# Edge stage of a graph network layer: all sixteen feature products of a step behind block 0 of the next step

## The reference, cut to what matters

```
def head(w1, bb1, w2, bb2, a1, aab1, a2, aab2):
    feats = jnp.maximum(x @ w1 + bb1, 0.0) @ w2 + bb2           # 256 -> 256 -> 64
    x_cat = jnp.concatenate([feats[row], feats[col], elem[:, None]], axis=1)
    hid = jnp.maximum(x_cat @ a1 + aab1, 0.0)                    # 129 -> 129
    e1 = (hid @ a2 + aab2)[:, 0]
    ...                                                          # softmax over the edges of a row
x = _layernorm(x + _L0_gnn_ref(...))
x = _layernorm(x + _L1_gnn_ref(...))
```

## Time and profile before

| what | us |
|---|---|
| median of 3 runs | 3850.22 |
| lowest and highest of them | 3822.89, 3856.89 |
| span of the profiled execution | 3543.6 |
| TensorE matmuls busy in it | 3149.9 (89%) |
| VectorE busy | 2727.7 (77%) |
| ScalarE busy | 1885.7 (53%) |
| GpSimd busy | 1802.6 (51%) |

### The profile page before, as it was taken

How to read it: one execution, slowest core, us unless ns; L and a number is a source line. 1 busy time by engine, 2 the same in 40 slices (tenths; PEclk the granted TensorE clock), 3 DMA queues, 4 the chain that set the end, 5 groups by cost and what they waited for, 6 DMA issues and landing times. The chain is left out here.

```text
span 3543.6 us, 66445 instructions
## 1 busy us (share of the span) xinstructions
PE 3149.9 (89%) x15901; PEld 2168.2 (61%) x15901; DVE 2727.7 (77%) x9307; ACT 1885.7 (53%) x4499; POOL 1802.6 (51%) x1827
## 2 busy tenths in 40 slices
PE   4987879885999997699999999999999999995775
PEld 2455546553555554477777777777777777773333
DVE  4988879774554544588888888888888888887997
ACT  2455557663665655344444444444444444443886
POOL 0046656665777774544444444444444444421777
PEclk9999999998999998799999999999999999997998
DMA  5889996444666665333333333333333333322885
GB/s 156 291 309 307 312 327 192 156 157 144 221 210 211 207 208 204 124 116 118 118 116 114 113 115 116 118 118 118 118 116 114 118 118 118 115 69 87 271 270 195
DMA packets 288948, 596.16 MB, mean 168 GB/s; under 512 B 41262, under 2 KB 198746, under 8 KB 288886
## 3 DMA queue, kind: packets, MB, share of 16 engines
q1 hardware_dynamic: 212774, 362.51, 30.6%
q0 software_dynamic: 75744, 232.45, 20.2%
q10 hardware_dynamic: 368, 0.52, 0.0%
HBM read 287.39 MB, written 322.05 MB: 172 GB/s over the span
## 5 line engine op out<-in xcount | busy, mean ns | idle before, releaser
L1029 PE MATMUL bank<-w_node,xT 128*128 128x384 f32 x1564 | 597.2, 506 | 80.2 <-ACT bank L617 79.6
L1218 POOL TENSOR_TENSOR u_hc<-u_hc 128x1536 f32<-128x1536 f32 x98 | 270.3, 2758 | 756.7 <-DVE u_h L1328 732.5
L1440 PE MATMUL bank<-xh,w1h 128*128 128x512 f32 x1568 | 537.7, 424 | 18.8 <-DVE xl L1357 14.9
L1270 ACT ACTIVATE hidT<-bank,b1c 128x512 f32<-128x512 f32 x392 | 268.7, 685 | 530.4 <-PE bank L1440 530.4
L1440 PE MATMUL bank<-xh,w1l 128*128 128x512 f32 x1568 | 494.1, 396 | 0.0
L1440 PE MATMUL bank<-xl,w1h 128*128 128x512 f32 x1568 | 493.0, 396 | 0.0
L1351 DVE TENSOR_SCALAR hidT<-bank,b1c 128x512 f32<-128x512 f32 x392 | 293.6, 749 | 199.7 <-PE bank L1440 196.7
L1029 PEld LDWEIGHTS bank<-w_node,xT 128*128 128x128 f32 x1564 | 286.5, 196 | 247.3 <-ACT bank L617 98.6
L1454 PE MATMUL bank<-hidT,w2f 128*64 128x256 f32 x3136 | 381.7, 385 | 0.9 <-issue 0.9
L617 ACT ACTIVATE bank<-bias_all 128x512 f32<-128x512 f32 x391 | 235.2, 602 | 250.8 <-DVE H L727 244.5
L1366 DVE STREAM_TRANSPOSE feat<-catT 32x256 f32<-32x256 f32 x784 | 342.7, 437 | 17.1 <-ACT catT L1279 3.0
(11 more groups left out here) (273 smaller groups left out, 6525.3 us busy)
## 6 DMA issues: line engine op xcount, KB each, us to landing
hc_tab<-H SPq DMA_DIRECT2D x78, 960.0 KB
hc_tab<-zero_row SPq DMA_DIRECT2D x15, 4992.0 KB
er<-edge_tab SPq DMA_DIRECT2D x98, 512.0 KB, 4.1
X<-in_x SPq DMA_DIRECT2D x78, 640.0 KB
out_x<-O SPq DMA_DIRECT2D x78, 640.0 KB
edge_tab<-u_x SPq DMA_DIRECT2D x98, 256.0 KB, 2.2
edge_tab<-feat SPq DMA_DIRECT2D x98, 256.0 KB, 2.2
u_hc<-hc_tab,u_idx POOLq DMA_INDIRECT x392, 4.4
```

Source lines behind the costliest of these rows:

```text
L1029: ins = t_.matmul(p[:, 0:384], xT[i % XR][:, c * P:(c + 1) * P], w_node[:, c, :], start=False, stop=c == 1, skip_group_check=True)
L1218: g.tensor_tensor(c, c, u_hc[s][:, :, MULT:MULT + 3].unsqueeze(3).to_broadcast([P, 4, 3, P]), ALU.mult).then_inc(u_scaled, 1)
L1270: a.activation(hidT[m][:, :], bank[2 + m % 2][:, :], ACT.Relu, bias=b1c[:, m:m + 1])\
L1440: ins = t_.matmul(bank[2 + m % 2][:, :], w[:, c, m * P:(m + 1) * P], xx[s][:, c, :], start=n == 0, stop=n == 5)
```

## The change

TensorE's list has one piece, features_0_1, with lag 2 behind hidden_0; it does both halves of step u-1, and the piece features_0 between blocks 6 and 7 is gone. The waits for all relus of the step and for the banks stand once, ahead of the first half. The relu of block 0 on ScalarE overwrites hidT 0, which the first half of the step before now reads later; so this relu waits for w2_ready of that step's second half. On ScalarE the piece features_0 moves from the end of the list to the place ahead of features_1, with lag 3. VectorE, GpSimd and SyncE are as they were.

```diff
                 def relu(u, m):
                     act.wait_ge(w1_ready, u * 8 + (m + 1))
+                    if m == 0 and after(u, 1):
+                        act.wait_ge(w2_ready, u * 2)
                     a.activation(hidT[m][:, :], bank[2 + m % 2][:, :], ACT.Relu, bias=b1c[:, m:m + 1])\
                         .then_inc(act_hid, 1)
...
-                skewed(act, US, 2, [(relu_0, 2), (features_1, 3), (seed_0, 3), (root, 0), (relu_2, 2), (norm, 0),
-                                    (relu_4, 2), (seed_1, 3), (high, 1), (relu_6, 2), (features_0, 2)])
+                skewed(act, US, 2, [(relu_0, 2), (features_0, 3), (features_1, 3), (seed_0, 3), (root, 0), (relu_2, 2),
+                                    (norm, 0), (relu_4, 2), (seed_1, 3), (high, 1), (relu_6, 2)])
...
                 def features(u, k):
-                    pe.wait_ge(act_hid, u * 4 + 2 * k + 2)
-                    pe.wait_ge(dve_hid, u * 4 + 2 * k + 2)
-                    if after(u, 1):
-                        pe.wait_ge(cat_ready, u * 4 + 2 * k - 2)
+                    if k == 0:
+                        pe.wait_ge(act_hid, u * 4 + 4)
+                        pe.wait_ge(dve_hid, u * 4 + 4)
+                        if after(u, 1):
+                            pe.wait_ge(cat_ready, u * 4)
...
-                def features_1(u, s):
+                def features_0_1(u, s):
+                    features(u, 0)
                     features(u, 1)
...
-                skewed(pe, US, 2, [(hidden_0, 1), (features_1, 2), (hidden_1, 1), (hidden_2, 1), (scores_0, 2),
+                skewed(pe, US, 2, [(hidden_0, 1), (features_0_1, 2), (hidden_1, 1), (hidden_2, 1), (scores_0, 2),
                                    (hidden_3_4, 1), (turn, 0), (hidden_5, 1), (scores_1, 2), (hidden_6, 1),
-                                   (features_0, 1), (hidden_7, 1)])
+                                   (hidden_7, 1)])
```

More of the change, by code:

```diff
@@ L1494, in hidden_6 @@
                     hidden(u, s, 6)
-                def features_0(u, s):
-                    features(u, 0)
                 def hidden_7(u, s):
```

## The result

The changed kernel takes 3966.68 us (median of 4 runs, 3957.06 to 3995.11), the kernel before 3844.37. The ratio is 1.0336 with a 95% interval of 1.0292 to 1.038: 3.4% slower, about 129 us (the two medians alone differ by 122). The forecast was 4028, with a range from 3990; the direction and the mechanism were right, the size was too large by 61 us in time and by 49 in the difference (178 against 129).

A forecast was written before the change was run, and what follows sets the result against it. TensorE, busy without a pause in the edge stage, was taken as the bound: 17.98 - 0.20 + 1.76 + 0.29 = 19.83 us a step, in total +178 us on the median 3850.22, giving 4028 us, range 3990 to 4065.

The forecast's parts named there:

- Term 1: TensorE's merged product group: eight products (1.87 us) move, one change-over in and out goes away, gaining 0.20 us a step.
- the loop: Group's start to end of block 5 on TensorE, 12.60 us, then VectorE's stretch with signal, 6.93: 19.53 against 17.98.
- Term 3: ScalarE's queue behind the new wait: relu of block 0 starts later, seed_0 and scores_0 are late, 0.29 us a step.
- Sum: Edge stage: 1.84 us a step, x 96 = 177, with the ends 178, added to the median 3850.22: 4028 us.
- Term 2: TensorE ahead of the merged group: waits 1.76 us a step for VectorE's relu of block 7.
- What was moved past: Other work on VectorE, GpSimd and SyncE (feat_0, gate and u_var, norm, high, stores): costs nothing at 19.8 us a step.
- B: Rival: TensorE's pauses in the edge stage cost clock as well; over 1% slower, chance 0.05.

The follow-up runs named there:

- the version with both repairs: Changed kernel, each half of the products waiting for its own relus, ScalarE's relu of block 0 for the first half only: ratio 0.992, in another sitting 0.9893.
- The two edits of ScalarE's part: Changed kernel with ScalarE's seed_0 ahead of the relu of block 0: ratio 1.0365; or with that relu waiting for the first half only: 1.0276.

## Why the prediction was right or wrong

What bounds each step was forecast rightly, and the sum built on it came out too large. The steps that failed are three sizes: the group of Term 1 and of the loop, taken at 3.75 us where it measured 3.60; the late scores of Term 3, taken at 0.29 where they measured about 0.14; and the carry-over in Sum, which left the edge stage out of the 307 us between span and median.

**Term 2 was right.** The wait of 1.76 us for the relu of block 7 came out as 1.66 to 1.68 of idle time, plus the 0.10 of changing over, VectorE's stretch at 6.93, and the loop closes over it. Splitting the wait, shortening the stretch and lengthening it (0.89 for 0.89) all moved the time as this says.

**What was moved past** cost nothing that shows: 12.58 from the group's start to the end of block 5 and VectorE's 6.93 add up to the whole period of 19.51.

**B, the loss of clock**, didn't happen behind any pause of 1.66 to 1.68 us. In the four traces of the changed kernel it did happen behind four longer ones: one of 1.94 us in the middle of the stage, one of 2.38 in its first steps, one of 2.00 and one of 2.01 in its last. The last section has the numbers.

**The group was sized wrong (Term 1 and the 12.60 of the loop).** I took 1.87 us for eight products and doubled it. But 1.88 contains the way out of the group once: thirty-two records take 3.60 us (2201.26 to 2204.86), not 3.75, and 3.67 in the version with both repairs. So a change-over costs 0.10 + 0.10 and another 0.08 to 0.15 hidden in the group's length, 0.28 to 0.35 rather than 0.20. The repaired version shows it without any wait: 17.98 - 17.70 = 0.28. Why the group behind a pause is the shorter one wasn't examined. Worth 0.15 x 96 = 14 us.

**The late scores were sized wrong (Term 3).** 0.29 a step was forecast. ScalarE's relu starts 0.11 after the group's end where I had taken the 0.25 of the earlier trace rows, so seed_0 is that much earlier, and the late scores cost only about 0.14 on average of both forms of the step (12.58 from group to end of block 5, against 12.60 - 0.15 without them). The two edits of ScalarE's part gave 0.12 to 0.13 back. Worth 14 us.

**The carry-over to the median failed (Sum).** I saw 307 us between the span and the median and wrote that the edge stage has no part in them. It has some 16, by the one trace of the kernel before from where runs take 3844: it already loses them there through its thin spare time, the changed kernel hardly does, and that much of the new loss was there before. The sum corrected: 178 - 14 - 14 - 16 = 134, measured 132 between the two spans and 129 by the ratio. All three went the same way, and the lower end of the range, 38 us below the forecast, has room for each alone but not for 44. The rest of the 61 us isn't the change's: with its fourth run the kernel before has a median of 3844.37 and not 3850.22, and the ratio says 129 where the two medians say 122. That the range missed by 23 us is in part the luck of these draws.

## What to carry to other kernels

Before a piece of work is moved on the engine that bounds, look at which wait it stands ahead of: a product that needs nothing new is the cover of the wait behind it, and merging two groups should not merge their waits. Measure the spare time of every wait that ends just in time (here 0.32 us of 17.98), since it says what a change may cost and where the small delays of another sitting will show. And when the profiled span is far from the median, as the 3543.6 here from 3850.22, the profile may be of other conditions, and even a stage that looks insensitive to them may change, as this one did by some 16 us.

## What the runs showed of the hardware that was not expected

TensorE's granted clock fell at the end of some short pauses, or right behind them, and not at others of the same length. In the changed kernel with two more transposes the second group follows a pause of 3.19 us and took 6.46 us in place of 3.67; the granted clock over 1740 to 1747 was 0.58. It was 1.00 until 1739, then 0.50 until 1745, 0.59 over the next us and 1.00 over the one after. The groups behind it follow pauses of 2.56 to 2.58 us, nearly all alike. Most of them kept the full clock, but the one right behind took 5.10, and five more, spread over the stage from 2091 to 3504 us, took 5.02 to 5.06, at a granted clock of 0.74 to 0.77 over 6 us each:

```profile
1740.16 6.46 PE L1465 MATMUL bank<-hidT,w2f 128*64 128x256 f32 x32 [3.19 <-issue]
1763.38 5.10 PE L1465 MATMUL bank<-hidT,w2f 128*64 128x256 f32 x32 [2.58 <-issue]
1785.17 3.67 PE L1465 MATMUL bank<-hidT,w2f 128*64 128x256 f32 x32 [2.56 <-issue]
...
2091.22 5.02 PE L1465 MATMUL bank<-hidT,w2f 128*64 128x256 f32 x32 [2.57 <-issue]
...
2439.37 5.02 PE L1465 MATMUL bank<-hidT,w2f 128*64 128x256 f32 x32 [2.56 <-issue]
```

The changed kernel itself shows the same at still shorter pauses. In one trace a group behind 1.94 us took 5.36, with a granted clock of 0.72 over 2180 to 2186; in another a group behind 1.96 us took 3.67, at 1.00:

```profile
2180.07 5.36 PE L1457 MATMUL bank<-hidT,w2f 128*64 128x256 f32 x32 [1.94 <-issue]
```

```profile
2689.18 3.67 PE L1457 MATMUL bank<-hidT,w2f 128*64 128x256 f32 x32 [1.96 <-issue]
```

In the first and last steps of the stage there are more. Behind 2.38 us a group took 5.36 (clock 0.72 over 1729 to 1735) and behind 2.32 in another trace 3.67. The last group of the stage took 3.67 in two traces, both behind 2.01; in the other two it took 5.29 behind 2.01 and 5.36 behind 2.00, with a clock of 0.72 over six us.

So the length of a pause alone doesn't say whether the clock falls; what else does, no run here shows. None of the pauses of 1.66 to 1.68 us was followed by a slower group, in any of its four traces.

And the same kernel takes 3545 us in one sitting and 3844 to 3887 in others, each run within 1% of the median of its sitting. Between the spans of 3540.8 and 3843.7, 227 us lie ahead of the edge stage (its first transpose at 1424.4 against 1651.7), 61 behind it and 15 inside. The four sittings ran on four chips; whether that makes the difference wasn't examined.
